# Layer 1 attention on one core: keys and queries turned by VectorE blocks and memory in place of TensorE transposes

## The reference

```python
k, q, v = x @ Wk + bk, x @ Wq + bq, x @ Wv + bv        # 1024 x 128 each
k = gk * k * rsqrt(mean(k * k, -1) + 1e-6)             # rmsnorm along the head's 128
q = gq * q * rsqrt(mean(q * q, -1) + 1e-6)
p = softmax(q @ k.T / sqrt(128))                       # 1024 x 1024
x = x + (p @ v) @ Wo_of_this_head
```

## Time and profile before

| | us |
|---|---|
| median of 3 runs | 3058.61 (3058.08 to 3059.47) |
| the profiled execution, its own time | 3054.36 |
| its span, first to last instruction | 3052.4 |
| PE busy / PEld busy | 2927.9 (96%) / 2630.0 (86%) |
| DVE busy | 2027.4 (66%) |
| ACT busy | 1544.3 (51%) |
| POOL busy | 1740.4 (57%) |
| granted TensorE clock, mean | 0.986 of full |

### The profile page before, as it was taken

One profiled execution on the slowest core, in us unless ns is written; L12 is line 12 of the kernel. 1 busy time (PEld: TensorE's weight loads), 2 busy tenths in 40 slices (PEclk: granted clock), 3 DMA queues, 4 the chain that ended last, 5 costly groups with the idle time before them and its releaser, 6 DMA issues. The chain is left out here.

```text
span 3052.4 us, 57532 instructions
## 1 busy us (share of the span) xinstructions
PE 2927.9 (96%) x17440; PEld 2630.0 (86%) x17440; DVE 2027.4 (66%) x3231; ACT 1544.3 (51%) x3019; POOL 1740.4 (57%) x1300
## 2 busy tenths in 40 slices
PE   7999999999999978899999999999999999986998
PEld 6999999999999957799989899898989999975886
DVE  5555656555565556677777777777777777775555
ACT  4443443344344323566666666666666666663222
POOL 5554554455455432466665666666666666654664
PEclk9999999999999989999999999999999999998999
DMA  3222222222222220456666565665656666566541
GB/s 114 66 77 86 65 66 85 78 65 74 86 68 65 71 73 23 153 194 208 197 201 207 192 204 195 205 204 197 203 192 205 199 204 202 193 197 185 153 141 45
DMA packets 310074, 430.57 MB, mean 141 GB/s; under 512 B 30464, under 2 KB 237312, under 8 KB 309888
## 3 DMA queue, kind: packets, MB, share of 16 engines
q1 hardware_dynamic: 272336, 294.82, 32.5%
q10 hardware_dynamic: 37680, 135.02, 11.1%
HBM read 276.63 MB, written 153.09 MB: 141 GB/s over the span
## 5 line engine op out<-in xcount | busy, mean ns | idle before, releaser
L1588 ACT ACTIVATE b_prob<-b_s_ps,b_shift 128x1024 f32<-128x1024 f32 x256 | 285.7, 1116 | 345.9 <-DVE b_shift L1738 338.7
L82 PE MATMUL b_pj_kq<-b_w_hi,xT_hi 128*128 128x384 f32 x1008 | 351.7, 349 | 23.8 <-DVE b_nat L1714 22.5
L83 PE MATMUL b_pj_kq<-b_w_lo,xT_hi 128*128 128x384 f32 x1008 | 342.8, 340 | 0.0
L84 PE MATMUL b_pj_kq<-b_w_hi,xT_lo 128*128 128x384 f32 x1008 | 342.6, 340 | 0.0
L1744 DVE STREAM_TRANSPOSE b_blocks<-b_prob 128x1024 f32<-128x1024 f32 x256 | 317.4, 1240 | 29.0 <-ACT b_prob L1588 28.5
L489 POOL TENSOR_TENSOR a_ga_lo<-a_gated,a_ga_hi 128x512 fp32r<-128x512 f32 x64 | 112.8, 1763 | 366.7 <-ACT a_ga_hi L577 366.7
L1510 POOL TENSOR_TENSOR b_pT_lo<-b_pT_lo,b_pT_hi 128x1024 fp32r<-128x1024 f32 x128 | 304.9, 2404 | 18.7 <-ACT b_pT_hi L1577 18.6
L1510 POOL TENSOR_TENSOR pT_lo<-pT_lo,pT_hi 128x1024 fp32r<-128x1024 f32 x128 | 305.0, 2406 | 13.1 <-ACT pT_hi L1577 13.1
L1495 POOL TENSOR_TENSOR b_rstd<-b_mean_sq,power 128x4 f32<-128x4 f32 x128 | 128.8, 1007 | 320.1 <-DVE b_mean_sq L1724 313.5
L1738 DVE TENSOR_REDUCE b_shift<-b_s_ps 128x1 f32<-128x1024 f32 x256 | 307.1, 1200 | 1.7 <-PE b_s_ps L84 1.7
L82 PE MATMUL a_pj<-b_w_hi,xT_hi 128*128 128x256 f32 x1024 | 295.5, 289 | 13.2 <-DVE xT_lo L825 11.0
(11 more groups left out here) (302 smaller groups left out, 9149.3 us busy)
## 6 DMA issues: line engine op xcount, KB each, us to landing
bounce<-b_blocks ACTq DMA_DIRECT2D x256, 512.0 KB, 3.5
pT_lo<-bounce SPq DMA_DIRECT2D x512, 128.0 KB, 3.1
b_pT_lo<-bounce SPq DMA_DIRECT2D x512, 128.0 KB, 2.9
b_w_raw<-in_w SPq DMA_DIRECT2D x32, 768.0 KB, 5.8
b_w_raw<-in_w SPq DMA_DIRECT2D x95, 256.0 KB, 3.2
k_bounce<-a_k_blocks SPq DMA_DIRECT2D x32, 512.0 KB, 4.0
a_k_raw<-k_bounce SPq DMA_DIRECT2D x128, 128.0 KB, 2.9
a_w_raw<-in_w SPq DMA_DIRECT2D x32, 256.0 KB, 3.1
```

What stands on the lines that cost most here:

```text
L82: pe.matmul(out, w_hi, x_hi, start=first, stop=False, skip_group_check=partial)
L83: pe.matmul(out, w_hi, x_lo, start=False, stop=False, skip_group_check=partial)
L84: return pe.matmul(out, w_lo, x_hi, start=False, stop=last, skip_group_check=partial)
L1588: act.activation(prob[t % 2][:, :], s_ps[t % 2][:, :], ACT.Exp, bias=shift[:, t:t + 1], accum_out=row_sum[:, t:t + 1]).then_inc(exp_done, 1)
```

## The change

Keys and queries of a batch no longer go through TensorE. VectorE turns them in 32x32 blocks (`turn_kq`, two instructions of 256 columns), ScalarE's queue writes the blocks to memory (`write_kq`), SP reads them back with four DMAs (`move_kq`) into `kq_raw`, and `kq_high` and `kq_low` then read SBUF; `q_lo` becomes two instructions, one for each tile. `transpose_kq` is gone and the freed half of `pj_kq` becomes a second projection bank, so `project_tile` waits for the tile before the last. Projections run two slots earlier (tiles 4 to 7 of head h + 1 in slots 0 to 3, tiles 0 to 3 of head h + 2 in slots 4 to 7), and `square`, `means`, `inverse_rms`, `scale_kq` one pair earlier (`prepared`); `turn_kq` and `write_kq` are in the odd slot behind them, `kq_high` and `kq_low` stay where they were. The first batch of `nat` is doubled. Weight splits move to slots 0, 1, 2; of the `v` splits two are in slot 5. SP's step now starts half a head earlier in the order of the moves. Three semaphores are merged into others.

```diff
-        pj, kq_ps = pj_kq[:, 0:HALF], pj_kq[:, HALF:].rearrange("p (k n) -> p k n", k=2)
+        pj = [pj_kq[:, 0:HALF], pj_kq[:, HALF:]]
...
         def project_bank(g, t):
-            return y_ps[:, 0:KQV] if peeled(g, 0) and t % 2 else pj[:, 0:KQV]
+            return pj[t % 2][:, 0:KQV]
...
         def projected(h, b, nxt, more, s):
-            if s < 6:
-                return (h + 1, 1 - b, s + 2) if nxt else None
-            return (h + 2, b, s - 6) if more else None
+            if s < 4:
+                return (h + 1, 1 - b, s + 4) if nxt else None
+            return (h + 2, b, s - 4) if more else None
+
+        def prepared(h, b, nxt, more, s):
+            i = s // 2 + 1
+            if i < NB:
+                return (h + 1, 1 - b, i) if nxt else None
+            return (h + 2, b, 0) if more else None
...
-        SPLITS = {1: 0, 2: 1, 4: 2}
+        def v_batches(h, b, cur, nxt, s):
+            if s == 1:
+                return ((h, b, 3),) if cur else ()
+            which = {5: (0, 1), 7: (2,)}.get(s, ())
+            return [(h + 1, 1 - b, i) for i in which] if nxt else ()
+
+        SPLITS = {0: 0, 1: 1, 2: 2}
...
+            def move_kq(g, i):
+                sp.wait_ge(kq_written, 16 * (NB * g + i + 1))
+                sp.sem_inc(room, 1)
+                wait(sp, kq_lo_done, NB * g + i - 1)
+                for c in range(GROUPS):
+                    sp.dma_start(kq_raw[i % 2][c * BLK:(c + 1) * BLK].rearrange("y r k u x -> y r (k u x)"),
+                                 kq_bounce[i % 2][:, :, c, :].rearrange("r y n -> y r n")).then_inc(kq_moved, 16)
...
-                if rest:
-                    move(h - 1, NT - 1)
-                for t in range(NT - 1):
+                for t in range(NT // 2, NT):
+                    if rest:
+                        move(h - 1, t)
+                    if t == 4 and cur:
+                        move_kq(h, 3)
+                    if t == 6 and nxt:
+                        move_kq(h + 1, 0)
+                for t in range(NT // 2):
                     if cur:
                         move(h, t)
+                    if t % 2 == 0 and nxt:
+                        move_kq(h + 1, t // 2 + 1)
...
             def kq_high(g, bg, i):
-                act.wait_ge(kq_tr, NB * g + i + 1)
+                act.wait_ge(kq_moved, 16 * GROUPS * (NB * g + i + 1))
                 wait(act, scored, NT * (g - 1))
-                act.activation(k_hi[bg][:, cut], kq_ps[:, 0, :], ACT.Copy)
-                act.activation(q_hi[bg][:, cut], kq_ps[:, 1, :], ACT.Copy, scale=gain[:, 0:1]).then_inc(kq_hi_done, 1)
+                act.activation(in_blocks(k_hi[bg][:, cut]), from_blocks(i, 0), ACT.Copy)
+                act.activation(in_blocks(q_hi[bg][:, cut]), from_blocks(i, 1), ACT.Copy,
+                               scale=gain[:, 0:1]).then_inc(kq_hi_done, 1)
+
+            def write_kq(g, i):
+                act.wait_ge(kq_blocked, 2 * (NB * g + i + 1))
+                wait(act, kq_written, 16 * (NB * g + i))
+                wait(act, kq_moved, 16 * GROUPS * (NB * g + i - 1))
+                act.dma_start(kq_bounce[i % 2][:, :, :, :].rearrange("r y c n -> (r y) (c n)"),
+                              kq_blocks[i % 2][:, :, :, :, :].rearrange("p c k u x -> p (c k u x)")).then_inc(
+                    kq_written, 16)
...
                     if nxt and s % 2:
                         kq_high(h + 1, 1 - b, s // 2)
+                    if s % 2 and ready:
+                        write_kq(ready[0], ready[2])
                     if cur:
                         exponent(h, b, s)
...
-                wait(pe, taken, NT * g + (t - 1 if peeled(g, 0) else t))
+                wait(pe, taken, NT * g + t - 1)
...
-                    if nxt and s % 2:
-                        transpose_kq(h + 1, s // 2)
...
             def kq_low(g, bg, i):
-                dve.tensor_tensor(k_lo[bg][:, cut], kq_ps[:, 0, :], f(k_hi[bg][:, cut]), ALU.subtract)
-                dve.scalar_tensor_tensor(out=q_lo[bg][:, cut], in0=kq_ps[:, 1, :], scalar=gain[:, 0:1],
-                                         in1=f(q_hi[bg][:, cut]), op0=ALU.mult,
-                                         op1=ALU.subtract).then_inc(kq_lo_done, 1)
+                dve.tensor_tensor(in_blocks(k_lo[bg][:, cut]), from_blocks(i, 0), f(in_blocks(k_hi[bg][:, cut])),
+                                  ALU.subtract)
+                for u in range(BATCH):
+                    one = slice(i * WIDE + u * P, i * WIDE + (u + 1) * P)
+                    last = dve.scalar_tensor_tensor(
+                        out=q_lo[bg][:, one].rearrange("p (r x) -> p r x", r=GROUPS), in0=kq_raw[i % 2][:, :, 1, u, :],
+                        scalar=gain[:, 0:1], in1=f(q_hi[bg][:, one]).rearrange("p (r x) -> p r x", r=GROUPS),
+                        op0=ALU.mult, op1=ALU.subtract)
+                last.then_inc(kq_lo_done, 1)
+
+            def turn_kq(g, bg, i):
+                dve.wait_ge(kq_scaled, NB * g + i + 1)
+                wait(dve, kq_written, 16 * (NB * g + i - 1))
+                for k in range(2):
+                    dve.transpose(kq_blocks[i % 2][:, :, k, :, :].rearrange("p c u x -> p u c x"),
+                                  nat_of(bg, i)[:, :, k * HD:(k + 1) * HD].rearrange(
+                                      "p u (c y) -> p u c y", c=GROUPS)).then_inc(kq_blocked, 1)
...
                 for s in range(NT):
                     q = quarter(h, b, cur, rest, s)
-                    if nxt and s % 2 == 0:
-                        means(h + 1, s // 2)
+                    ready = prepared(h, b, nxt, more, s)
+                    if s % 2 == 0 and ready:
+                        means(ready[0], ready[2])
+                    if s % 2 and ready:
+                        turn_kq(*ready)
                     if projected(h, b, nxt, more, s):
                         take(*projected(h, b, nxt, more, s))
```

More of the change, by code:

```diff
@@ L1313, in l1_attention @@
         bias_sb = [sb(f"bias{b}", [P, KQV]) for b in range(2)]
-        nat = [sb(f"nat{i}", [P, BATCH, KQV]) for i in range(NB)]
+        nat_first = [sb(f"nat0{b}", [P, BATCH, KQV]) for b in range(2)]
+        nat_rest = [sb(f"nat{i}", [P, BATCH, KQV]) for i in range(1, NB)]
+        kq_blocks = [sb(f"kq_blocks{i}", [P, GROUPS, 2, BATCH, BLK]) for i in range(2)]
+        kq_bounce = [nc.dram_tensor(f"kq_bounce{i}", (GROUPS, BLK, GROUPS, 2 * BATCH * BLK), F32) for i in range(2)]
+        kq_raw = [sb(f"kq_raw{i}", [P, GROUPS, 2, BATCH, BLK]) for i in range(2)]
         sq = sb("sq", [P, BATCH, 2, HD])
@@ L1513, in step @@
                 for s in range(NT):
-                    if nxt and s % 2 == 0:
-                        inverse_rms(h + 1, 1 - b, s // 2)
-                    if v_batch(h, b, cur, nxt, s):
-                        v_low(*v_batch(h, b, cur, nxt, s))
+                    if s % 2 == 0 and prepared(h, b, nxt, more, s):
+                        inverse_rms(*prepared(h, b, nxt, more, s))
+                    for which in v_batches(h, b, cur, nxt, s):
+                        v_low(*which)
                     if split_batch(h, cur, rest, s):
@@ L1536, in _, with square @@
                 ln_in.scalar_high(act, ln_banks, t)
-            def square(g, i):
+            def square(g, bg, i):
                 act.wait_ge(taken, NT * g + BATCH * (i + 1))
-                wait(act, summed, NB * g + i)
-                act.activation(sq[:, :, :, :].rearrange("p t k d -> p t (k d)"), nat[i][:, :, 0:2 * HD],
+                wait(act, means_done, 2 * (NB * g + i))
+                act.activation(sq[:, :, :, :].rearrange("p t k d -> p t (k d)"), nat_of(bg, i)[:, :, 0:2 * HD],
                                ACT.Square).then_inc(squared, 1)
@@ L1566, in scale_kq @@
                     for k in range(2):
-                        part = nat[i][:, u, k * HD:(k + 1) * HD]
+                        part = nat_of(bg, i)[:, u, k * HD:(k + 1) * HD]
                         last = act.activation(part, part, ACT.Copy, scale=rstd[bg][:, BATCH * i + u, k:k + 1])
@@ L1592, in step @@
                 if peeled(h, -1):
-                    act.wait_ge(gain_ready, 1)
+                    act.wait_ge(gain_and_bias, 1)
                 for s in range(NT):
[L1595 to L1598, removed]
+                    ready = prepared(h, b, nxt, more, s)
+                    if s % 2 == 0 and ready:
+                        square(*ready)
+                    for which in v_batches(h, b, cur, nxt, s):
+                        v_high(*which)
                     q = quarter(h, b, cur, rest, s)
@@ L1604, in step @@
                             prob_hi(*split_batch(h, cur, rest, s), part)
-                    if nxt and s % 2 == 0:
-                        scale_kq(h + 1, 1 - b, s // 2)
+                    if s % 2 == 0 and ready:
+                        scale_kq(*ready)
                     if rest and s == 0:
@@ L1639, in project_tile @@
                 last.then_inc(proj, 1)
```

(18 more changed lines are left out.)

40 lines of the change are left out of this document (20 added, 20 removed).

## The result

| | us |
|---|---|
| before, median | 3058.35 |
| after, median of 4 runs | 3153.42 (3151.9 to 3155.12) |
| ratio after to before, 95% interval | 1.0313 (1.0295 to 1.0331) |
| the profiled execution of after, its span | 3150.7 |
| TensorE busy | 2888.9 (92%) |

The account below looks back on a forecast made before the run. The prediction took a closed loop through ScalarE's and VectorE's queues as the bound: 0.53 + 0.13 = 0.66 us a pair over 124 batches is +82, plus 14 for the start, +96 on 3054.4, so 3150 us; range 3100 to 3215.

Parts of the forecast that it names:

- The ring: Closed loop through ScalarE's and VectorE's in-order queues, exponent to exponent, without TensorE; claimed to bound the kernel, 11.77 us a pair.
- TensorE's part: Four transposes a batch (0.44 us) and the wait on the one projection bank vanish from TensorE; costed at nothing.
- `turn_kq`, +0.53 a pair: Two block transposes on VectorE ahead of `take`, 0.35 us each, less 0.17 idle: +0.53 us a pair (0.45 to 0.67).
- `kq_low`, +0.13: On VectorE, one 256-wide `q_lo` becomes two of 128 columns: +0.13 us a pair (0 to +0.31).
- `kq_high`, nothing: On ScalarE, `kq_high` reads SBUF and was claimed to take the same 0.78 us, so no added time.
- The start, +14: Step -1, before any scores cover the new round trip through memory: +14 us in all (5 to 20).
- The spare of 3.3 us of the round trip: Keys and queries written to memory and read back: landed at about 2056, needed by `kq_high` at 2059.2, 3.3 us spare.
- my signs of being wrong: Trace signs listed beforehand: a period under 11.6, maxima waiting for TensorE, or `kq_high` waiting for a DMA in the steady part.
- The rival "late round trip": `kq_high` on ScalarE waits for its memory reads, everything behind it held; about 3350 us at one and a half times; chance 0.07.
- The rival "TensorE is the bound after all": TensorE sets the time, so both its savings reach the end: 2994 us, faster; chance 0.10.

## Why the prediction was right

Forecast 3150, measured 3153.42, and for the reason given, though the closeness is in part luck: several terms were off and nearly cancel. Point by point, by its steps:

- **The ring is the bound.** Shown: two reordered instructions open it (3013 and 3019), and work of one size costs 40 us inside it and nothing outside. TensorE's own need was below the 11.77 that I gave as its most: at most 11.62 a pair.
- **TensorE's part costs and brings nothing.** Shown: the transposes back on TensorE, 3154 against 3155. The next late thing was named as the output bank at some 1.1 us a pair, and it is: 143.5 us in 120 waits, 1.2 each. Its busy share fell to 90% and not 94%, and that was a slip of mine: my own 11.33 in a pair of 11.93 + 0.66 is 90%.
- **`turn_kq`, +0.53 a pair.** Its size was right (a step of 0.34 each), what it pushes was not: +0.39 in the trace. I took up only the 0.17 us of idle in the earlier trace rows. That idle is counted from the reciprocal's end, while back to back the two overlap: the step from the reciprocal's start to the long transpose shrank from 0.33 to 0.06, so 0.27 was there to be taken up. This term was too large by 0.14, and on the old kernel alone it came to 40 us in place of my 66.
- **`kq_low`, +0.13**: 0.14. Its `k_lo`, now with two SBUF operands, is however no longer of one length. This pair of rows of after is from the pair before the one above:

```profile
2013.44 0.73 POOL L1540 TENSOR_TENSOR b_v_lo<-b_nat,b_v_hi 128x256 fp32r<-128x256 f32 x1
2013.76 0.69 DVE L1771 TENSOR_TENSOR b_k_lo<-b_kq_raw,b_k_hi 128x256 fp32r<-128x256 f32 x1 [1.46 <-ACT b_q_hi L1587]
```

- **`kq_high`, nothing**: it cost 0.07, and its place behind the write 0.05 more. These two missing terms and the one above that was too large nearly cancel, so the 0.66 a pair came out exactly in the pair shown, by luck in its parts. The mean pair grew by 0.70.
- **The start, +14**: 8.2. I took the landing time of the busy steady part; in the quiet start the first write of keys and queries was issued at 1212.35 and its reads at 1214.45, so it landed in 2.1 us and not 3.5. The chain was another one, too. I priced a batch of step -1 at 8.5 us by its round trip, but no `kq_high` there waits for its reads. ScalarE idles for POOL's `b_rstd` ahead of `scale_kq`, and the batches follow each other every (1239.35 - 1217.85) / 3 = 7.17 us:

```profile
1217.85 0.40 ACT L1586 ACTIVATE b_k_hi<-b_kq_raw 128x256 fp32r<-128x256 f32 x1
...
1223.79 1.28 ACT L1616 ACTIVATE b_nat<-b_nat,b_rstd 128x128 f32<-128x128 f32 x4 [4.00 <-POOL b_rstd L1533]
...
1239.35 0.42 ACT L1586 ACTIVATE b_k_hi<-b_kq_raw 128x256 fp32r<-128x256 f32 x1
```

- **The spare of 3.3 us of the round trip** holds in most slots, but not in the one beside the weight load, where 16 waits add up to 37.6 us. So one of my signs of being wrong, `kq_high` waiting for a DMA in the steady part, did show. It does not carry the loss: most of these waits pass under the wait for the long transpose that stands at the same place anyway, and only some 8 us of them lie beyond the usual step from `write_blocks` to `kq_high`. I had costed a write at its median landing, and judged the DMA engines by their mean share, and not beside the one large load of each head: in the two windows from 2040 to 2050 us, behind such a load, the profile gives their share as full, 1.02 and 1.09. The rival "late round trip" was nearer than 7 in 100 suggests: putting the write 4 us later brings it about, and putting the load later does it for the probabilities.

The rival "TensorE is the bound after all" fell with the runs above: it needed the ring to be under 11.33.

## What to carry to other kernels

When an engine is 99% busy, look at who waits for whom before relieving it: here VectorE's `maxima` waited 0.9 us in 1500 for the scores of a TensorE that was so busy, and a walk from exponent to exponent closed without touching TensorE. In this ring the order of instructions in the in-order queues was worth more (140 us on the changed kernel) than what the change added to their lengths (some 80): an instruction that nothing in the ring needs (`kq_low`) must not stand ahead of one that it does need (`maxima`). A wait put on a queue, even for something produced in idle time elsewhere, holds all that is queued behind it.

## What the runs showed of the hardware that I had not expected

- A 128x256 TENSOR_TENSOR on VectorE with both operands in SBUF took 0.42 us alone and up to 0.93 in the steady part; the one of 0.69 above ran while POOL worked on `v_lo`. With one PSUM operand the same instruction always took 424 to 427 ns in the kernel before. The traces separate the cases cleanly. From 1300 to 2800 us of after, all 27 `k_lo` of 0.45 us and more overlapped a `v_lo` on POOL, which reads two SBUF operands as well, and none of the 90 shorter ones did; before, 59 of 119 overlapped a `v_lo` and none was longer than 0.43. So a POOL instruction at the same time goes with the longer one when both operands are in SBUF, and not when one is in PSUM. No run moved `v_lo` by itself.
- A 256 KB write that landed in 2.1 us on idle DMA engines and in 3.7 in the median took 6.6 beside a 768 KB load. The mean DMA share of that kernel, 0.67, does not show it; that of the 10 us around the write does, 0.93 and 1.01 in the two halves.
